# A one-core recurrent block with a quantised gate, in 16 chunks: fewer products on TensorE, transposes in longer groups, layernorm sums at another place

## What is computed

```python
xn = layernorm(x)
# branch s
a = dwconv_causal3(rmsnorm(xn) ) @ pw.T + b + xn            # x1
hid, gate = split(rmsnorm(a) @ gru_w.T)                      # 2 x 256
a = scan(h = (1 - sig(gate)) * h + sig(gate) * g(hid)) + a   # along the 512 tokens, x2
s = gelu(rmsnorm(a) @ w1.T + b1) @ w2.T + b2 + a             # 256 -> 1024 -> 256
# branch g
q = fp4(v): blocks of 16 values, scale = max|v| / 6, rounded to the grid 0 .. 6
h = silu(q(xn) @ q(w_gate).T) * (q(xn) @ q(w_up).T)          # 256 -> 704
g = silu(q(h) @ q(w_down).T)                                 # 704 -> 256
out = x + s * g
```

## Time and profile before

| | |
|---|---|
| three runs | 1085.59 us median, 1084.41 to 1086.84 |
| profiled execution | 1085.26 us, span 1083.5 us, mean granted TensorE clock 0.997 |
| busy PE, DVE, ACT, POOL | 98%, 86%, 56%, 14% of the span |
| DMA | 31.45 MB, mean 29 GB/s |

### The profile page before, as it was taken

How to read it: one execution, slowest core, us unless ns; L and a number is a source line. 1 busy time by engine, 2 the same in 40 slices (tenths; PEclk the granted TensorE clock), 3 DMA queues, 4 the chain that set the end, 5 groups by cost and what they waited for, 6 DMA issues and landing times. The chain is left out here.

```text
span 1083.5 us, 18319 instructions
## 1 busy us (share of the span) xinstructions
PE 1061.8 (98%) x6954; PEld 967.9 (89%) x6954; DVE 934.5 (86%) x1720; ACT 607.3 (56%) x967; POOL 147.5 (14%) x123
## 2 busy tenths in 40 slices
PE   7899999999999999999999999999999999999998
PEld 6788989989898998989999898998989899898998
DVE  6978988989888898988889898898989889898895
ACT  5564464564746547474654747455574645647452
POOL 1230101112020110201111010111101011120010
PEclk9999999999999999999999999999999999999999
DMA  7000001010010101001010010101001010100110
GB/s 248 1 21 1 1 2 59 1 60 1 1 59 1 59 1 47 13 2 59 1 60 1 21 40 1 59 1 60 1 1 59 1 59 1 59 1 2 39 40 21
DMA packets 29365, 31.45 MB, mean 29 GB/s; under 512 B 1120, under 2 KB 28512, under 8 KB 29280
## 3 DMA queue, kind: packets, MB, share of 16 engines
q1 hardware_dynamic: 28448, 29.43, 8.7%
q10 hardware_dynamic: 832, 0.87, 0.2%
HBM read 21.90 MB, written 8.39 MB: 28 GB/s over the span
## 5 line engine op out<-in xcount | busy, mean ns | idle before, releaser
L990 PE MATMUL gu_ps<-gu_hi,xq_hi 128*128 128x352 f32 x512 | 168.3, 329 | 0.0
L990 PE MATMUL gu_ps<-gu_lo,xq_hi 128*128 128x352 f32 x512 | 165.9, 324 | 0.0
L990 PE MATMUL gu_ps<-gu_hi,xq_lo 128*128 128x352 f32 x512 | 165.7, 324 | 0.0
L990 PE MATMUL w_ps<-w_hi,act_hi 128*128 128x256 f32 x480 | 140.1, 292 | 0.0
L990 PE MATMUL w_ps<-w_hi,act_lo 128*128 128x256 f32 x480 | 135.1, 281 | 0.0
L990 PE MATMUL w_ps<-w_lo,act_hi 128*128 128x256 f32 x480 | 134.9, 281 | 0.0
L990 PE MATMUL w_ps<-dn_hi,hqt_hi 128*128 128x256 f32 x384 | 116.6, 304 | 2.0 <-DVE hqt_lo L519 2.0
L990 PE MATMUL w_ps<-dn_hi,hqt_lo 128*128 128x256 f32 x384 | 108.5, 283 | 0.0
L990 PE MATMUL w_ps<-dn_lo,hqt_hi 128*128 128x256 f32 x384 | 108.4, 282 | 0.0
L818 ACT ACTIVATE g<-w_ps 128x256 f32<-128x256 f32 x64 | 24.7, 385 | 147.7 <-PE w_ps L990 147.6
L496 DVE TENSOR_TENSOR hid<-sl,gu_ps 128x704 f32<-128x704 f32 x64 | 56.8, 887 | 58.8 <-PE gu_ps L990 58.2
(11 more groups left out here) (136 smaller groups left out, 2703.6 us busy)
## 6 DMA issues: line engine op xcount, KB each, us to landing
x_in<-x_dram SPq DMA_DIRECT2D x16, 512.0 KB, 5.8
x_res<-x_dram SPq DMA_DIRECT2D x16, 512.0 KB, 5.0
out_dram<-o SPq DMA_DIRECT2D x15, 512.0 KB, 3.5
act<-w_t_dram SPq DMA_DIRECT2D x1, 1024.0 KB, 11.3
w_f<-w_t_dram SPq DMA_DIRECT2D x1, 1024.0 KB, 13.8
w_f<-w_down_dram SPq DMA_DIRECT2D x1, 704.0 KB, 9.4
hid<-w_gate_dram SPq DMA_DIRECT2D x1, 640.0 KB, 5.9
hid<-w_up_dram SPq DMA_DIRECT2D x1, 640.0 KB, 9.3
```

Source lines behind the costliest of these rows:

```text
L990: done = M.matmul(psum, l, r, start=first and i == 0, stop=last and i == len(terms) - 1)
```

## The change

1. `pointwise` becomes a product in two parts: `pw` is split once into `pw_hi` and `pw_lo`, ACT makes `y_hi` (`front_y_high`), DVE `y_lo` (`front_y_low`, two 128x512), and PE does twelve float32r matmuls instead of four fp32 ones. Its eight transposes stand together ahead of them.
2. The last 64 columns of `hq` are written twice (`fp4_hidden_values`, one more DVE instruction of 128x64), so that the sixth transposed tile holds them on both halves of the partitions. `hidden_low` becomes two instructions: 128x640 into `hqt_lo`, and 64x128, which puts the low part on the lower half of the tile in `hqt_hi`. `down` does that tile with two matmuls instead of three, 17 in all. The down weights are laid out alike.
3. The transposes of x2b at the head of each `ff2` are a function of their own (`ff2_open`) and are put beside other transposes. In `body` PE now does `down(c - 1, 3)` ahead of `sum_squares(2c + 1)`, `ff2` of tile 3 between that and the spread, and `front_xc(c + 1)` and the opening of tile 2 right behind the spread.
4. The layernorm sums are taken apart: `front_stats(c + 2)` (four statistics) at the end of `body(c)`, `front_moments` after `hidden_values(c - 1, 2)`, from body 2 on. `front_rows` moves ahead of the second `clamp_sums`. On SP the load of the inputs moves ahead of the store.
5. `gelus_low` is cut 4 and 4 instead of 5 and 3. `output_sum` is as it was.
6. ACT: `front_y` after the first gelu, `front_y_high` ahead of the last two.
7. In `first` the low parts of w1 and w2 are made by DVE (`ff_low`) instead of POOL, the first recurrence comes before weight tile 3 instead of after it, the weight tiles 3 to 5 are interleaved with `ff1`, the counts of filler matmuls (`keep_busy`) differ, and several tiles share homes.

```diff
             load(2)
             with sp.Fori(0, B - 3) as i:
+                load(i + 3)
                 store(i)
-                load(i + 3)
...
-            def front_moments(c):
+            def fp4_hidden_values(dst, rounded):
+
+                n, last = NBI * FP4_BLOCK, NFULL * P // FP4_BLOCK
+                fp4_values(dst[:, 0:n], NBI, rounded)
+                return V.scalar_tensor_tensor(blocks(dst[:, n:KI * P], NBI - last),
+                                              blocks(q_m[:, NFULL * P:n].bitcast(BF16), NBI - last),
...
-                    V.scalar_tensor_tensor(y[:, k, 2:L], tap(0), dww[:, k, 0:1], y[:, k, 2:L],
-                                           ALU.mult, ALU.add).then_inc(y_ready, 1)
+                    front_tap(c, k)
+
+            def front_y_low(c):
+
+                for k in range(KD):
+                    dve.wait_ge(yhi_ready, KD * c + k + 1)
+                    V.tensor_tensor(y_lo[:, k, :], y[:, k, :], y_hi[:, k, :].bitcast(F32),
...
                 dve.wait_ge(dn_done, T * c + t)
-                V.tensor_tensor(hqt_lo[:], hqt_ps, hqt_hi[:].bitcast(F32), ALU.subtract).then_inc(hqtlo_ready, 1)
+                V.tensor_tensor(hqt_lo[:], hqt_ps[:, 0:NFULL, :], hqt_hi[:, 0:NFULL, :].bitcast(F32), ALU.subtract)
+
+                twin = hqt_hi[LAST:P, NFULL, :]
+                V.tensor_tensor(twin, hqt_ps[LAST:P, NFULL, :], twin.bitcast(F32),
+                                ALU.subtract).then_inc(hqtlo_ready, 1)
 
...
-                gelus_low(c - 1, range(5))
+                gelus_low(c - 1, range(4))
                 hidden(c, 0)
...
                 ratios = fp4_ratios(hid[:, 2, :], NBI, scales)
                 clamp_sums(c * 2, w_ps[:, 0, :])
                 hidden_values(c - 1, 2, fp4_round(NBI, ratios))
-                gelus_low(c - 1, range(5, KF))
+                if front and c > 1:
+                    front_moments(carried["stats"])
+                gelus_low(c - 1, range(4, KF))
                 hidden(c, 2)
                 scaled(c * 2, x1, w_ps[:, 1, :], (x1_ready, KD * (c + 1)))
                 scales = hidden_scales(c - 1, 3)
@@ -674,30 +721,34 @@
                 dve.wait_ge(dve_step, ratios)
                 hidden(c, 3)
                 hidden_values(c - 1, 3, fp4_round(NBI, ratios))
-                if front:
-                    front_moments(c + 1)
+                if front and c == 1:
+                    front_moments(front_stats(c + 1))
                 recurrence(c, 0)
                 recurrence(c, 1)
                 hidden_low(c - 1, 3)
                 add_squares(c * 2 + 1)
                 output(c - 1, 0, w_ps[:, 0, :])
-                clamp_sums(c * 2 + 1, gu_ps[:, 0, 0, :])
                 if front:
                     front_rows(c + 1)
+                clamp_sums(c * 2 + 1, gu_ps[:, 0, 0, :])
+                output(c - 1, 1, w_ps[:, 1, :])
                 scales = hidden_scales(c, 0)
                 scaled(c * 2 + 1, x1, gu_ps[:, 0, 1, :], (x2_ready, KD * (c + 1)))
                 scaled_low(c * 2 + 1)
-                output(c - 1, 1, w_ps[:, 1, :])
                 ratios = fp4_ratios(hid[:, 0, :], NBI, scales)
                 hidden_values(c, 0, fp4_round(NBI, ratios))
                 output(c - 1, 3, w_ps[:, 3, :])
                 output(c - 1, 2, w_ps[:, 2, :])
                 if front:
-                    front_fp4_values(c + 1, front_fp4_ratios(c + 1))
+                    ratios = front_fp4_ratios(c + 1)
                     front_taps(c + 1)
+                    front_fp4_values(c + 1, fp4_round(T * NBD, ratios))
+                    front_y_low(c + 1)
                     carried["ratios"] = fp4_ratios(hid[:, 1, :], NBI, hidden_scales(c, 1))
                     hidden_low(c, 0)
                     front_fp4_low(c + 1)
+                    if c + 2 < B:
+                        carried["stats"] = front_stats(c + 2)
 
...
+            def front_y_high(c):
+
+                for k in range(KD):
+                    act.wait_ge(y_ready, KD * c + k + 1)
+                    act.wait_ge(pw_done, KD * c)
+                    act.wait_ge(x2_ready, KD * c)
+                    A.copy(y_hi[:, k, :], y[:, k, :]).then_inc(yhi_ready, 1)
...
-                for j in range(KF // 2):
+                gelus(c, (0,))
+                if front:
+                    front_y(c + 1)
+                gelus_high(c, (0,))
+                for j in range(1, KF // 2):
                     gelus(c, (j,))
                     gelus_high(c, (j,))
                 if front:
-                    front_y(c + 1)
-                    gelus(c, range(KF // 2, KF))
+                    gelus(c, range(KF // 2, KF - 2))
+                    front_y_high(c + 1)
+                    gelus(c, range(KF - 2, KF))
                     hq_columns(c, 0)
                     front_xq(c + 1)
                     gelus_high(c, range(KF // 2, KF))
...
 
             def pointwise(c):
+                pe.wait_ge(y_ready, KD * (c + 1))
                 for e in range(KD):
-                    pe.wait_ge(y_ready, KD * (c + 1))
                     for t in range(T):
                         M.matmul(w_ps[:, e, t * P:(t + 1) * P], xn[:, t, e * P:(e + 1) * P], ident[:],
                                  is_transpose=True, start=t == 0, stop=False)
+                pe.wait_ge(yhi_ready, KD * (c + 1))
+                pe.wait_ge(ylo_ready, KD * (c + 1))
+                for e in range(KD):
                     for k in range(KD):
-                        last = product(w_ps[:, e, :], pw[:, k, e * P:(e + 1) * P], y[:, k, :], False, k == KD - 1)
+                        last = product(w_ps[:, e, :], (pw_hi[:, k, e * P:(e + 1) * P], pw_lo[:, k, e * P:(e + 1) * P]),
+                                       (y_hi[:, k, :], y_lo[:, k, :]), False, k == KD - 1)
                     last.then_inc(pw_done, 1)
 
...
             def down(c, t, bank=w_ps[:, 2, :]):
                 pe.wait_ge(hqthi_ready, T * c + t + 1)
                 pe.wait_ge(hqtlo_ready, T * c + t + 1)
-                for k in range(KI):
-                    last = product(bank[:, 0:D], (hqt_hi[:, k, :], hqt_lo[:, k, :]),
-                                   (dn_hi[:, k, :], dn_lo[:, k, :]), k == 0, k == KI - 1)
-                last.then_inc(dn_done, 1)
+                for k in range(NFULL):
+                    product(bank[:, 0:D], (hqt_hi[:, k, :], hqt_lo[:, k, :]), (dn_hi[:, k, :], dn_lo[:, k, :]),
+                            k == 0, False)
+
+                M.matmul(bank[:, 0:D], hqt_hi[:, NFULL, :], dn_lo[:, NFULL, :], start=False, stop=False)
+                M.matmul(bank[:, 0:D], hqt_hi[:, NFULL, :], dn_hi[:, NFULL, :], start=False,
+                         stop=True).then_inc(dn_done, 1)
 
             def gru(c, k):
...
 
-            def ff2(c, t, bank, free):
+            def ff2_open(c, t, bank, free):
+
+                pe.wait_ge(x2b_ready, KD * (c + 1))
+                pe.wait_ge(*free)
+                tok = slice(t * P, (t + 1) * P)
+                for k in range(KD):
+                    M.matmul(bank[:, k * P:(k + 1) * P], x2b[:, k, tok], ident[:], is_transpose=True,
+                             start=k == 0, stop=False)
+
+            def ff2(c, t, bank):
 
                 pe.wait_ge(acthi_ready, KF * (c + 1))
                 pe.wait_ge(actlo_ready, KF * (c + 1))
-                pe.wait_ge(x2b_ready, KD * (c + 1))
-                if free:
-                    pe.wait_ge(*free)
                 tok = slice(t * P, (t + 1) * P)
-
-
-                for k in range(KD):
-                    M.matmul(bank[:, k * P:(k + 1) * P], x2b[:, k, tok], ident[:], is_transpose=True,
-                             start=k == 0, stop=False)
                 for j in range(KF):
                     last = product(bank[:, 0:D], (act_hi[:, j, tok], act_lo[:, j, tok]), (w2_hi[:, j, :], w2_lo[:, j, :]),
                                    False, j == KF - 1)
...
                 gru(c, 0)
                 gru(c, 1)
                 hq_transposes(c - 1, 3, (g_ready, T * c - 1))
-                ff2(c - 1, 0, w_ps[:, 0, :], (ss_ready, 2 * c + 1))
-                ff2(c - 1, 1, w_ps[:, 1, :], (xs_ready, KD * (2 * c + 1)))
+                ff2_open(c - 1, 0, w_ps[:, 0, :], (ss_ready, 2 * c + 1))
+                ff2_open(c - 1, 1, w_ps[:, 1, :], (xs_ready, KD * (2 * c + 1)))
+                ff2(c - 1, 0, w_ps[:, 0, :])
+                ff2(c - 1, 1, w_ps[:, 1, :])
+                down(c - 1, 3)
                 sum_squares(c * 2 + 1, gu_ps[:, 0, 0, :], (coef_ready, KD * c + 1))
-                down(c - 1, 3)
+                ff2_open(c - 1, 3, w_ps[:, 3, :], (hqtlo_ready, T * c))
+                ff2(c - 1, 3, w_ps[:, 3, :])
                 spread_scale(c * 2 + 1, gu_ps[:, 0, 1, :], (cand_ready, KD * c + 1))
-                ff2(c - 1, 3, w_ps[:, 3, :], (hqtlo_ready, T * c))
-                ff2(c - 1, 2, w_ps[:, 2, :], (g_ready, T * c))
-                ff1(c, range(KF // 2))
```

(7 more changed lines are left out.)

216 lines of the change are left out of this document (124 added, 92 removed).

## The result

The changed kernel takes 1137.39 us (median of 4 runs, 1131.59 to 1138.61), the kernel before 1085.0: a ratio of 1.047, 95% interval 1.043 to 1.051. It is 52 us slower. The forecast was 1130, the range 1105 to 1150. The profiled execution took 1137.88 us, its span 1136.1.

What follows compares the result with a forecast made beforehand. The prediction took PE to bound the kernel, busy 63.75 of 63.97 us a period. It summed 1085.3 + 14 x (3.9 + 1.5 - 1.6) - 0.6 - 1.1 - 7 = 1129.8, say 1130 us, range 1105 to 1150.

Steps and rivals of the forecast that it cites:

- The wait: At the first spread, bodies 2 to 15: PE stands still 3.9 us for POOL's power, held behind its late sum.
- The clock: Behind each of the 14 waits at the first spread: half clock costs PE 1.5 us, ends 0 and 2.4.
- Rival A: At the first spread the wait comes but the clock stays up: 1109 us, chance 0.15.
- PE's savings: PE's work per period (pointwise, down, second spread, joined transposes) shrinks by 1.6 us, to a period of 62.4 us.
- The sum over the periods: Over 14 periods: 14 x (3.9 + 1.5 - 1.6) = 53.2 us added, less 0.6 because body 15 has no moments.
- The start: Chunk 0, up to body 1: earlier recurrence and less work on POOL save 7 us, bounds 0 and -12.
- The tail: At the end: six shorter downs and no late second spread in body 15 save 1.1 us.
- Both are covered: DVE's added 2.1 us a period fits 6.3 idle; ACT's two copies of about 0.6 us fit 27 idle.
- The lateness: hidden_low of tile 2 would come 0.8 us late a period if DVE's cover goes, unless a larger wait hides it.
- rival C: POOL's sum is not in the way of the power, so the kernel is faster: 1054 to 1066 us, chance 0.06.
- Rival B: POOL's sum lets all act_lo pieces pass first, 1.2 us more in each of 14 periods: 1147 us, chance 0.15.

Runs made afterwards that it cites:

- e1: The changed kernel with POOL's output sum waiting for 4 act_lo pieces of the next chunk, not 5: 1084.02 us, ratio 0.9985.
- e2: The changed kernel with the act_lo pieces cut 5 and 3, the sum's wait for the 5th kept: 1082.46 us, ratio 0.9975.
- e3: The kernel before with only the act_lo pieces cut 4 and 4 in place of 5 and 3: 1151.1 us, ratio 1.059.
- e5: The changed kernel with 14 identity matmuls put into PE's wait ahead of the first spread: 1116.79 us, ratio 1.0278.
- e12: e9 with PE's old order at the second squares (sums of squares, down of tile 3, spread, ff2 of tile 3): 1090.87 us, ratio 1.0045.
- e7: e2 with, in the tail, all eight act_lo pieces on DVE directly behind tile 0's low parts: 1080.84 us, ratio 0.9937.
- e10: e9 with, in the tail, all act_lo pieces behind tile 0's low parts and tile 2's low parts ahead of tile 3's rounding: 1062.51 us, ratio 0.9779.
- e9: e2 with the layernorm stats and moments back together behind tile 3's hidden values, as before the change: 1066.75 us, ratio 0.9811.
- e4: The changed kernel with POOL's output sum waiting for all 8 act_lo pieces, not 5: 1159.84 us, ratio 1.0676.

## Why the prediction was right, and where it was not

- **The wait (3.9 us; measured 3.67) was right, and so was its cause.** From the first of the late pieces to the spread the forecast had 5.03 us (565.57 to 570.6), the trace 4.96. The sum does wait for the piece in flight: by the record, from 448.70, it takes 2.67 us, 0.26 more than in the earlier trace rows, and the power is 1.46 and not 1.23. e1 and e2 take the wait away by either end of it, and e3 makes it in the kernel before.
- **The clock (14 x 1.5 = 21 us) was right as a sum, with some luck.** Against the period in which the clock stayed up (66.20 us, 62.51 without its wait), nine periods lose 1.5 to 1.7 us to it, two lose 2.5, and two lose nothing: 19.5 us. The fourteenth wait's half clock falls into the tail, 1.6 us. So a fall costs more than 1.5, and not every wait brings one. e5 puts the mean at 1.47 by itself. Rival A (1109 us) fell as a whole and came true for two waits of 14.
- **PE's savings (-1.6) were right**: 1.57 by the table. Pointwise takes 3.65 us up to the down (496.45 to 500.10), 4.31 before; the second spread has no wait:

```profile
475.87 0.60 PE L1117 MATMUL gu_ps<-ident,xs 128*128 128x128 f32 x4
...
479.37 0.60 PE L1125 MATMUL gu_ps<-ident,inv_rms 128*128 128x128 f32 x4
...
496.45 1.04 PE L1084 MATMUL w_ps<-ident,xn 128*128 128x128 f32 x8
497.25 0.48 PE L1061 MATMUL w_ps<-y_hi,pw_hi 128*128 128x512 f32 x1
```

- **The sum over the periods** was 14 x 3.8 = 53.2 us, less 0.6 for body 15; measured 14 x (67.60 - 63.98) = 50.7, without the last wait's half clock, which the forecast had in it. The last wait is 3.14 us, 0.53 less than the others, as the missing moments have it.
- **The start (-7) was too hopeful**: the first spread of body 1 comes at 114.82 for 118.98, -4.2. The recurrent layer no longer waits (its first matmul is at 37.95 with no idle time), but comes 2.0 us later than before, and PE waits 1.7 us for xq (0.4 before), which no step of the forecast had. The value lies within the bounds given.
- **The tail (-1.1) is the term that failed**: 68.8 us from the last first spread to the end before, 74.9 after, +6.1. The step "the tail has six shorter downs, and body 15 no late second spread" left out that an ff2 tile now stands ahead of the second spread. In chunk 15 nothing is gained by that, and all that DVE does behind the spread comes later: the last act_lo piece ends 45.3 us after the first spread before, 48.4 in e1, 49.5 after the change, where half clock behind the last wait comes on top (1.6 us: in e5, without it, 47.9). PE waits 3.56 us for it at the first ff2, in place of 1.74, and then the clock falls. e12 bears it out, though it was made for the periods: PE's old order gives 2.3 us of the tail back. e7 and e10 show that DVE's order alone gives 3.0 and 5.0.
- In all: 1085.3 - 4.2 + 50.7 + 6.1 = 1137.9, the profiled time. The start's 2.8 and the tail's 7.2 us are what lies between that and the forecast, less 1.9 of the periods (50.7 for 53.2 - 0.6). Of the tail's 7.2 the fourteenth fall of the clock is 1.6, so the tail's own miss is 5.6.
- **"Both are covered" was wrong**, and did not show. DVE's additions were taken as +2.1 us against 6.3 of idle time. Its busy time grows by 3.2 (59.19 in e1, 56.03 in the earlier trace rows), of which 0.76 is q_wide held up beside POOL's sum. And idle time elsewhere in the period was no cover, since from y_lo to the down of tile 2 there is next to none. The lateness was reckoned at 0.8 us a period and is 1.5 (e1). So rival C had its price wrong: with the sum out of the way the kernel takes 1082 to 1084 us, and not 1054 to 1066. That number needs the moments moved back as well (e9, 1066.75).
- **Rival B** (the sum lets all pieces pass) is what e4 builds: 1160 us, not 1147. Against 1.2 us a chunk the place costs 1.5, of which 0.5 is clock. The Trainium skill, page "SBUF — State Buffer", section "Who interferes with whom", says that the order of issue decides who blocks. The rows agree as far as they go: the sum was issued while the second of four pieces was under way and came in behind it, and the third, issued later, was held (2.83 us for 0.69).

Not tried: why the clock stayed up behind two of the 14 waits is open. It is not the wait's length, which is 3.67 to 3.69 us in 13 of them. In the 3.5 us behind the second to the seventh wait the mean granted clock is 0.51, 0.57, 0.64, 0.70, 0.50 and 1.00, and behind the eighth to the thirteenth it is the same again within 0.01. The mean clock of the four runs is 0.976 in three and 0.983 in the one that took 1131.59 us. The 2.8 us of the start are open too.

## What to carry to other kernels

A wait on a count is a wait on a place in another engine's list: whoever cuts or moves that list has to look for all who wait on its counts, and for what stands behind them. Idle time of an engine covers an addition only where it lies in the same stretch of the engine's list. Ask which stretch has no gap, and put additions outside it. An order that helps in every period can hurt in the tail, where there is nothing behind it to overlap. When a large stall hides a smaller one, price what comes to light before expecting the savings back.

## What the runs showed of the hardware

- A wait of PE for POOL's power of 2.9 to 4.7 us was followed by half clock 40 times of 42 (after the change, e3, e4), and two of 3.69 and 3.67 us (after the change, at 589.35 and 995.53) were not. A fall cost 1.4 to 1.8 us as a rule and 2.0 to 3.0 where the low level lasted longer. Shorter waits of 1.96 us (chunk 0, before) and 2.13 us (the tail of e12) were followed by it as well. Waits of up to 1.1 us in each period (e1, e12) and of 1.74 us (e7) were not.
- Filler matmuls kept the clock up: 14 products of the identity in each wait gave back 20.6 us of 52 (e5).
- POOL's power of 128 x 4 elements takes 1.02 us without a DVE piece beside it (e4) and 1.46 beside DVE's pieces, and its sum of 128 x 1024 takes 2.34 and 2.67. It goes the other way too: beside the sum a DVE piece took 2.83 us for 0.69, and q_wide, 128 x 44, took 0.95 for 0.19 (e1). So a step's length on either engine depends on what the other does.
